# Two halves of a linear layer, walked together instead of one after the other

## The chip, the cores and the metric

The kernel runs on one core of one Trainium2 chip. The metric is device time in microseconds of one execution. A profiled execution of the same program gives the trace from which the rows below are read.

## The reference, cut to what matters

For each of 64 batch entries a 64 x 64 matrix W is picked out of 16 by an index, and mixes the 64 channels of x (1024 long). The result y goes through a linear layer with a weight that is stored as 6-bit numbers, four of them in three words, and x is added at the end:

```python
W = weights[condition]                                # 64 of 16 matrices, 64 x 64
y = jnp.einsum('bct,bcd->bdt', x, W)                  # x: 64 x 64 x 1024
w = (unpacked.astype(jnp.float32) - zero_point) * scale   # 1024 x 1024, a scale and zero point per row
out = x + jnp.einsum('bsk,nk->bsn', y, w) + bias
```

## The kernel before

Two batch entries make a tile of 128 rows, so there are 32 tiles, numbered t = i * 4 + j in loops of RING = 4. For each tile the engines do the following.

- SyncE (SP) loads x and, by the two indices, the mixing matrices (`reload`, seven tiles ahead in the steady part), and stores the two halves of the outputs (`store`), which wait for `o_ready[h]`.
- TensorE runs the mix (`mix`, L249): eight chunks of x as stationary operand against a block-diagonal matrix, into y_ps. It appears as 16 matmuls in the trace. A small sum follows (`sum_y`, L262, two short matmuls). Then comes the linear layer.
- ScalarE copies y_ps to y_hi, rounded (L355), and VectorE subtracts to get the rest, y_lo (L434). Both halves of the number are multiplied with the weight, so that little precision is lost. ScalarE also sums x (L346); POOL adds the bias to x (L540); VectorE adds the zero point's share (`residual`, L443).
- VectorE finishes a half of the outputs with two instructions: it scales o_ps into o_sb (`scale_out`, L454), which sets the semaphore `scaled[h]`, and adds the residual (`add_residual`, L462), which sets `o_ready[h]`. In each tile it does half 0 first, then half 1.

The linear layer (`linear` and `products`, L274 to L288) multiplies the eight chunks of y with qT, 1024 wide, in two halves of 512 outputs (H = 2), each of which fills one bank of o_ps. A half walks all eight chunks, each with y_hi and y_lo: 16 matmuls, with the piece of y as stationary operand and 512 columns of qT moving. Half 0 waits for the tile's y_lo and for `scaled[0]` of the tile before, half 1 for `scaled[1]` of the tile before. A matmul's data type is fp32r; each `nc.tensor.matmul` asks for a load of its stationary operand and a matmul.

The order on TensorE is written out by hand. A warm-up of 20 matmuls (L300) is followed by a prologue in which mixes, transposes of the weight (L270) and the first linears alternate. In the steady part, `step` (L290) does the mix and the sum of the tile three ahead and then the linear of tile j, both halves. The last steps (L330) have no mix left from tile 29 on; tile 31 does half 0 and then two quarter-wide pieces (`last_pieces`, L334). y_ps has two buffers, o_ps has one per half, o_sb has two, and x, y_hi, y_lo and resid have four.

Of the kernel before, what the change touches and what calls it, by code (L numbers as in the profile page):

```python
# [31 lines left out]
def adaln_ffn(nc: bass.Bass, x, cond, weights, qweight, scale, zero, bias, out):  # L32
    B, C, K = x.shape
    NCOND, _, S = weights.shape
    N, KP = qweight.shape
    assert C == S == P // 2 and N == K
    G = KP // 3
    KT = K // P
    NT = N // P
    H = 2  # L40
    NH = N // H
    TILES = B // 2
    RING = 4
# [8 lines left out]
    with ExitStack() as ctx:  # L52
        def sb(name, shape, dt):
            return ctx.enter_context(nc.sbuf_tensor(name, shape, dt))

        def psum(name, shape, dt):
            return ctx.enter_context(nc.psum_tensor(name, shape, dt))

        def sem(name):
            return ctx.enter_context(nc.semaphore(name))  # L60
# [5 lines left out]
        y_hi = sb("y_hi", [P, RING, KT, P], F32R)  # L66
        y_lo = sb("y_lo", [P, RING, KT, P], F32R)
        qT = sb("qT", [P, KT, N], F32R)
# [16 lines left out]
        o_ps = psum("o_ps", [P, H, NH], F32)  # L85
# [31 lines left out]
        y_lo_ready = sem("y_lo_ready")  # L117
# [5 lines left out]
        o_ps_ready = [sem(f"o_ps_ready{h}") for h in range(H)]  # L123
        scaled = [sem(f"scaled{h}") for h in range(H)]
# [5 lines left out]
        def x_arrived(eng, j, i):  # L130

            eng.wait_ge(x_loaded[j % RING], (i + j // RING + 1) * 16)
# [3 lines left out]
        def _(sp):  # L136
# [36 lines left out]
            def store_last():  # L173
                t = TILES - 1
                store(t % RING, t // RING, 0)
                for n, (_, col, width) in enumerate(last_pieces):
                    sp.wait_ge(o_ready[1], t + 1 + n)
                    sp.dma_start(out_rows[t * P:(t + 1) * P, col:col + width],
                                 o_sb[:, t % 2, col:col + width]).then_inc(o_stored[1][t % 2], 16)
# [58 lines left out]
        @block.tensor  # L238
        def _(pe):
            def mix(j, i):  # L240

                t = i * RING + j
                slot = j % RING
                x_arrived(pe, j, i)
                pe.wait_ge(w_loaded[slot], (i + j // RING + 1) * 32)
                if not isinstance(t, int) or t >= 2:
                    pe.wait_ge(y_lo_ready, (t - 1) * 2)
                for kt in range(KT):
                    last = nc.tensor.matmul(y_ps[:, j % 2, kt, :], x_sb[:, slot, kt * P:(kt + 1) * P],  # L249
                                            w_sb[:, slot, :], start=True, stop=True)  # L250
                    if kt % (KT // 2) == KT // 2 - 1:
                        last.then_inc(y_ps_ready, 1)

            def sum_y(j, i):

                t = i * RING + j
                slot = j % RING
                pe.wait_ge(w_stacked[slot], (i + j // RING + 1) * 32)
                pe.wait_ge(xsum_ready, t * 2 + 2)
                if not isinstance(t, int) or t >= 1:  # L260
                    pe.wait_ge(ysum_ready, t * 2)
                nc.tensor.matmul(ysum_ps[0:S, 2 * slot:2 * slot + 2], w_stack[:, slot, :], xsum[:, slot, :],  # L262
                                 start=True, stop=True).then_inc(ysum_ps_ready, 1)

            def transpose_q(n):
                pe.wait_ge(q_cast, n + 1)
                if n >= 2:
                    pe.wait_ge(qt_ready, n - 1)
                for kt in range(KT):
                    last = nc.tensor.transpose(qt_banks[n % 2][:, kt, :], q_bf[:, n % 4, kt * P:(kt + 1) * P],  # L270
                                               ident[:])
                last.then_inc(qt_ps_ready, 1)

            def linear(j, i, h):  # L274
                t = i * RING + j
                if h == 0:
                    pe.wait_ge(y_lo_ready, t * 2 + 2)
                if not isinstance(t, int) or t >= 1:
                    pe.wait_ge(scaled[h], t)
                products(o_ps[:, h, :], h * NH, NH, j % RING).then_inc(o_ps_ready[h], 1)  # L280

            def products(bank, col, width, slot):
                for kt in range(KT):
                    for part in (y_hi, y_lo):
                        last = nc.tensor.matmul(bank, part[:, slot, kt, :], qT[:, kt, col:col + width],  # L285
                                                start=(kt == 0 and part is y_hi),
                                                stop=(kt == KT - 1 and part is y_lo))
                return last  # L288

            def step(j, i, mixes=True):  # L290
                if mixes:
                    mix(j + LEAD, i)
                    sum_y(j + LEAD, i)
                for h in range(H):
                    linear(j, i, h)


            pe.wait_ge(warm_ready, 1)
            for _ in range(WARMUP):
                nc.tensor.matmul(ysum_ps[:], warm[:, 0:P], warm[:], start=True, stop=True)  # L300
            mix(0, 0)
            sum_y(0, 0)
            pe.wait_ge(ident_ready, 1)
            for n in range(NT // 2):
                transpose_q(n)
            mix(1, 0)
            pe.wait_ge(qt_ready, NT // 2)
            linear(0, 0, 0)
            sum_y(1, 0)
            mix(2, 0)  # L310
            sum_y(2, 0)
            transpose_q(4)
            transpose_q(5)
            linear(1, 0, 0)
            transpose_q(6)
            transpose_q(7)
            linear(2, 0, 0)
            mix(3, 0)
            sum_y(3, 0)
            pe.wait_ge(qt_ready, NT)  # L320
            for j in range(3):
                linear(j, 0, 1)
                mix(j + RING, 0)
                sum_y(j + RING, 0)
            for h in range(H):
                linear(3, 0, h)
            with pe.Fori(1, TRIPS - 1) as i:
                for j in range(RING):
                    step(j, i)
            for j in range(RING - 1):  # L330
                step(j, TRIPS - 1, mixes=j + LEAD < RING)
            linear(RING - 1, TRIPS - 1, 0)
            pe.wait_ge(scaled[1], TILES - 1)
            for bank, col, width in last_pieces:  # L334
                products(bank, col, width, RING - 1).then_inc(o_ps_ready[1], 1)
# [235 lines left out]
```

## Time and profile before

| | us |
|---|---|
| median of 3 runs | 331.95 |
| lowest, highest | 331.39, 332.85 |
| span of the profiled execution (first to last instruction) | 331.5 |
| TensorE matmuls busy | 319.6 |
| TensorE loads busy | 268.9 |
| VectorE busy | 211.4 |
| ScalarE busy | 127.8 |
| POOL busy | 78.3 |

The profiled execution's own time is not listed beside its span. Engine names in the rows: PE is TensorE's matmuls and PEld its loads of stationary operands, which overlap; DVE is VectorE, ACT is ScalarE, POOL is GpSimd, SP is SyncE. The start of a matmul is recorded and its end is modelled, so the distance of two starts says more than a length. L285 is the linear's matmul, L249 that of the mix. PEclk is the granted TensorE clock as a share of 2.4 GHz.

### The profile page before, as it was taken

How to read it: one execution, taken by the hardware profiler on the slowest of the kernel's cores; microseconds unless marked ns; L12 is line 12 of the kernel's file. 1: busy time of each engine (PE TensorE's matmuls, PEld its weight loads, DVE VectorE, ACT ScalarE, POOL GpSimd, SP SyncE). 2: the span in 40 equal slices, each digit the busy share in tenths (PEclk: the TensorE clock that was granted, in tenths of full speed). 3: DMA queues.
4: the chain of work that ended last, by engine and by line, in shares of the span. 5: the costliest groups of instructions: out<-in, count | busy, mean ns of one | idle time of the engine just before them, and what ended most of it. 6: DMA issues, size and time to landing. Idle time of an engine off the chain costs nothing.

```text
span 331.5 us, 5520 instructions
## 1 busy us (share of the span) xinstructions
PE 319.6 (96%) x1700; PEld 268.9 (81%) x1700; DVE 211.4 (64%) x262; ACT 127.8 (39%) x265; POOL 78.3 (24%) x39
## 2 busy tenths in 40 slices
PE   8797699999999999999999999999999999999995
PEld 3685588888888888888888888888888888888885
DVE  3459984666566676665666766656667666566563
ACT  4659157543333444433334444333344443330000
POOL 1006505222112222221122222211222222112000
PEclk9779599999999999999999999999999999999999
DMA  5895055625333333233333332433333321111112
GB/s 174 237 317 190 10 176 166 199 83 198 125 114 104 131 132 104 100 134 122 115 116 117 132 111 94 135 121 116 115 119 130 109 96 63 55 40 65 63 73 86
DMA packets 25805, 40.52 MB, mean 122 GB/s; under 512 B 11970, under 2 KB 12226, under 8 KB 25794
## 3 DMA queue, kind: packets, MB, share of 16 engines
q1 hardware_dynamic: 25794, 40.39, 36.5%
q8 instruction: 5, 0.08, 0.1%
q14 instruction: 6, 0.05, 0.0%
HBM read 23.59 MB, written 16.78 MB: 122 GB/s over the span
## 4 chain that ended last, share of the span: by engine, by line
PE 91%; DVE 3%; SPq 2%; DMA 1%; ACT 1%; issue 1%
PE o_ps L285 71%; PE y_ps L249 17%; PE ysum_ps L262 2%; DMA q_raw<-in_L_ffn_qweight_dram 1%; DVE q_bf L426 1%; DVE q_int L419 1%; DVE q_int L421 1%; ACT junk L346 1%; PE o_ps L270 1%; PE y_ps L285 1%; SPq L182 0%; SPq L148 0%; SPq L153 0%; SPq L144 0%; SPq L139 0%
## 5 line engine op out<-in xcount | busy, mean ns | idle before, releaser
L285 PE MATMUL o_ps<-qT,y_hi 128*128 128x512 f32 (+1 forms) x512 | 203.7, 399 | 0.0
L285 PE MATMUL o_ps<-qT,y_lo 128*128 128x512 f32 (+1 forms) x512 | 199.5, 390 | 0.0
L540 POOL TENSOR_TENSOR resid<-x_sb,bias_bc 128x1024 f32<-128x1024 f32 x32 | 77.1, 2414 | 221.6 <-DVE o_sb L462 195.7
L285 PEld LDWEIGHTS o_ps<-qT,y_hi 128*128 128x128 f32 x512 | 97.1, 190 | 20.0
L285 PEld LDWEIGHTS o_ps<-qT,y_lo 128*128 128x128 f32 x512 | 97.2, 190 | 19.1
L454 DVE TENSOR_TENSOR o_sb<-o_ps,scale_bc 128x512 f32<-128x512 f32 x63 | 43.6, 691 | 92.8 <-PE o_ps L285 92.8
L355 ACT ACTIVATE y_hi<-y_ps 128x512 fp32r<-128x512 f32 x64 | 38.2, 599 | 157.6 <-PE y_ps L249 157.6
L346 ACT ACTIVATE junk<-x_sb 64x1024 bf16<-64x1024 f32 x64 | 67.6, 1057 | 1.6
L249 PEld LDWEIGHTS y_ps<-w_sb,x_sb 128*128 128x128 f32 x512 | 63.6, 196 | 2.4
L249 PE MATMUL y_ps<-w_sb,x_sb 128*128 128x128 f32 x512 | 64.1, 280 | 0.0
L443 DVE SCALAR_TENSOR_TENSOR resid<-zs_bc,ysum,resid 128x1024 f32<-128x1024 f32 x32 | 60.4, 1886 | 0.0
L434 DVE TENSOR_TENSOR y_lo<-y_ps,y_hi 128x512 fp32r<-128x512 f32 x64 | 44.0, 691 | 12.0 <-ACT y_hi L355 9.1
L462 DVE TENSOR_TENSOR o_sb<-o_sb,resid 128x512 f32<-128x512 f32 x63 | 43.6, 692 | 2.3
L346 ACT ACTIVATION_READ_ACCUMULATOR junk<-x_sb 64x1 f32 x64 | 11.8, 185 | 0.0
L365 ACT ACTIVATE ysum<-ysum_ps 64x1 f32<-64x1 f32 x64 | 10.1, 158 | 2.3 <-PE ysum_ps L262 1.5
L262 PEld LDWEIGHTS ysum_ps<-xsum,w_stack 128*64 128x64 f32 x64 | 6.1, 134 | 5.0 <-issue 1.4
L262 PE MATMUL ysum_ps<-xsum,w_stack 128*64 128x2 f32 x64 | 8.8, 207 | 0.8 <-issue 0.8
L417 DVE TENSOR_SCALAR q_int<-q_raw 128x256 int16<-128x256 int16 x8 | 3.7, 459 | 7.8 <-DMA q_raw<-in_L_ffn_qweight_dram 7.8
L300 PE MATMUL ysum_ps<-warm 128*128 128x512 bf16 x20 | 7.0, 530 | 1.2 <-DVE warm L470 1.2
L270 PE MATMUL o_ps<-ident,q_bf 128*128 128x128 bf16 x32 | 3.3, 265 | 4.9 <-DVE q_bf L426 4.9
L270 PEld LDWEIGHTS o_ps<-ident,q_bf 128*128 128x128 bf16 x32 | 2.5, 119 | 5.3 <-DVE q_bf L426 5.3
L300 PEld LDWEIGHTS ysum_ps<-warm 128*128 128x128 bf16 x20 | 2.5, 129 | 5.2 <-issue 3.3
(26 smaller groups left out, 45.3 us busy)
## 6 DMA issues: line engine op xcount, KB each, us to landing
x_sb<-in_x_dram SPq DMA_DIRECT2D x32, 512.0 KB, 3.3
out_dram<-o_sb SPq DMA_DIRECT2D x63, 256.0 KB, 2.0
q_raw<-in_L_ffn_qweight_dram SPq DMA_DIRECT2D x8, 384.0 KB, 5.4
w_sb<-in_L_cond_weights_dram SPq DMA_DIRECT2D x64, 16.0 KB, 2.0
w_stack<-in_L_cond_weights_dram SPq DMA_DIRECT2D x64, 16.0 KB, 2.1
scale_bc<-_L_ffn_weight_scale_dram SPq DMA_DIRECT2D x1, 512.0 KB, 6.1
zs_bc<-n_weight_zero_point_dram SPq DMA_DIRECT2D x1, 512.0 KB, 7.5
bias_bc<-in_L_ffn_bias_dram SPq DMA_DIRECT2D x1, 512.0 KB, 8.4
```

The source lines that it names most:

```text
L249: last = nc.tensor.matmul(y_ps[:, j % 2, kt, :], x_sb[:, slot, kt * P:(kt + 1) * P], w_sb[:, slot, :], start=True, stop=True)
L262: nc.tensor.matmul(ysum_ps[0:S, 2 * slot:2 * slot + 2], w_stack[:, slot, :], xsum[:, slot, :], start=True, stop=True).then_inc(ysum_ps_rea ...
L285: last = nc.tensor.matmul(bank, part[:, slot, kt, :], qT[:, kt, col:col + width], start=(kt == 0 and part is y_hi), stop=(kt == KT - 1 and ...
L300: nc.tensor.matmul(ysum_ps[:], warm[:, 0:P], warm[:], start=True, stop=True)
L346: nc.scalar.activation(junk[rows, :], x_sb[rows, j % RING, :], ACT.Copy, accum_out=xsum[rows, j % RING, half:half + 1]).then_inc(xsum_read ...
L355: nc.scalar.activation(y_hi[:, j % RING, chunks, :], y_ps[:, j % 2, chunks, :], ACT.Copy).then_inc(y_hi_ready, 1)
L365: nc.scalar.activation(ysum[half * S:(half + 1) * S, j % RING:j % RING + 1], ysum_ps[0:S, col:col + 1], ACT.Copy).then_inc(ysum_ready, 1)
L434: nc.vector.tensor_tensor(y_lo[:, j % RING, chunks, :], y_ps[:, j % 2, chunks, :], y_hi[:, j % RING, chunks, :].bitcast(F32), ALU.subtract ...
L443: nc.vector.scalar_tensor_tensor(resid[:, j % RING, :], zs_bc[:], ysum[:, j % RING:j % RING + 1], resid[:, j % RING, :], ALU.mult, ALU.add ...
L454: nc.vector.tensor_tensor(o_sb[:, j % 2, cols], o_ps[:, h, :], scale_bc[:, cols], ALU.mult).then_inc(scaled[h], 1)
L462: nc.vector.tensor_tensor(o_sb[:, j % 2, cols], o_sb[:, j % 2, cols], resid[:, j % RING, cols], ALU.add).then_inc(o_ready[h], 1)
L540: nc.gpsimd.tensor_tensor(resid[:, j % RING, :], x_sb[:, j % RING, :], bias_bc[:], ALU.add).then_inc(xbias_ready, 1)
```

## The change

A new function, `linear_both`, takes the place of two calls of `linear` in the steady steps and for tile 3. It waits for y_lo and for both `scaled` semaphores first, then walks the chunks once: at each chunk and for each of y_hi and y_lo it issues the matmul of half 0 and then that of half 1, with the same stationary operand. The last matmul of each half sets that half's `o_ps_ready`. Tiles 3 to 30 go through it; tiles 0 to 2 and tile 31 keep `linear` and `products`.

```diff
--- before.py
+++ after.py
@@ -271,6 +271,21 @@
                                                ident[:])
                 last.then_inc(qt_ps_ready, 1)
 
+            def linear_both(j, i):
+                t = i * RING + j
+                pe.wait_ge(y_lo_ready, t * 2 + 2)
+                for h in range(H):
+                    pe.wait_ge(scaled[h], t)
+                for kt in range(KT):
+                    for part in (y_hi, y_lo):
+                        for h in range(H):
+                            last = nc.tensor.matmul(o_ps[:, h, :], part[:, j % RING, kt, :],
+                                                    qT[:, kt, h * NH:(h + 1) * NH],
+                                                    start=(kt == 0 and part is y_hi),
+                                                    stop=(kt == KT - 1 and part is y_lo))
+                            if kt == KT - 1 and part is y_lo:
+                                last.then_inc(o_ps_ready[h], 1)
+
             def linear(j, i, h):
                 t = i * RING + j
                 if h == 0:
@@ -291,8 +306,7 @@
                 if mixes:
                     mix(j + LEAD, i)
                     sum_y(j + LEAD, i)
-                for h in range(H):
-                    linear(j, i, h)
+                linear_both(j, i)
 
 
             pe.wait_ge(warm_ready, 1)
@@ -322,8 +336,7 @@
                 linear(j, 0, 1)
                 mix(j + RING, 0)
                 sum_y(j + RING, 0)
-            for h in range(H):
-                linear(3, 0, h)
+            linear_both(3, 0)
             with pe.Fori(1, TRIPS - 1) as i:
                 for j in range(RING):
                     step(j, i)
```

## Rows read from the trace of the kernel before

**Rows 1.** Page, table of engines: busy us, share of the span, instructions.
```profile
PE 319.6 (96%) x1700; PEld 268.9 (81%) x1700; DVE 211.4 (64%) x262; ACT 127.8 (39%) x265; POOL 78.3 (24%) x39
```

**Rows 2.** Chain of waits, steady part: start us, length us, what, how many instructions.
```profile
201.93 1.78 PE y_ps L249 x16
...
203.93 7.48 PE o_ps L285 x32
211.41 1.78 PE y_ps L249 x16
```

**Rows 3.** Timeline of TensorE, one tile: start us, length us, engine, line, operation.
```profile
196.33 0.39 PE L285 MATMUL o_ps<-qT,y_hi 128*128 128x512 f32 x1
...
197.92 0.39 PE L285 MATMUL o_ps<-qT,y_lo 128*128 128x512 f32 x1
198.15 0.39 PE L285 MATMUL o_ps<-qT,y_hi 128*128 128x512 f32 x1
...
201.54 0.39 PE L285 MATMUL o_ps<-qT,y_lo 128*128 128x512 f32 x1
```

**Rows 4.** Timeline of all engines at that tile's end; in brackets idle time and releaser.
```profile
201.97 0.69 DVE L454 TENSOR_TENSOR o_sb<-o_ps,scale_bc 128x512 f32<-128x512 f32 x1 [2.21 <-PE o_ps L285]
202.70 0.69 DVE L462 TENSOR_TENSOR o_sb<-o_sb,resid 128x512 f32<-128x512 f32 x1
...
203.49 0.69 DVE L434 TENSOR_TENSOR y_lo<-y_ps,y_hi 128x512 fp32r<-128x512 f32 x1
203.53 2.40 POOL L540 TENSOR_TENSOR resid<-x_sb,bias_bc 128x1024 f32<-128x1024 f32 x1 [7.07 <-DVE o_sb L462]
...
203.85 0.50 PE L285 MATMUL o_ps<-qT,y_hi 128*128 128x512 f32 x1
...
204.19 0.39 PE L285 MATMUL o_ps<-qT,y_lo 128*128 128x512 f32 x1
```

**Rows 5.** Timeline of VectorE, same tile and the next.
```profile
198.35 0.69 DVE L454 TENSOR_TENSOR o_sb<-o_ps,scale_bc 128x512 f32<-128x512 f32 x1 [0.81 <-PE o_ps L285]
...
205.00 2.02 DVE L443 SCALAR_TENSOR_TENSOR resid<-zs_bc,ysum,resid 128x1024 f32<-128x1024 f32 x1
```

**Rows 6.** Groups by line and form: count, busy us, mean ns, idle before.
```profile
L285 PEld LDWEIGHTS o_ps<-qT,y_lo 128*128 128x128 f32 x512 | 97.2, 190 | 19.1
...
L300 PE MATMUL ysum_ps<-warm 128*128 128x512 bf16 x20 | 7.0, 530 | 1.2 <-DVE warm L470 1.2
...
L300 PEld LDWEIGHTS ysum_ps<-warm 128*128 128x128 bf16 x20 | 2.5, 129 | 5.2 <-issue 3.3 <-DVE warm L470 1.2
...
L270 PEld LDWEIGHTS qt_ps<-ident,q_bf 128*128 128x128 bf16 x32 | 1.8, 99 | 2.1 <-DVE q_bf L426 1.8 <-issue 0.3
```

**Rows 7.** Timeline of VectorE early on, independent instructions in a row.
```profile
41.11 0.69 DVE L462 TENSOR_TENSOR o_sb<-o_sb,resid 128x512 f32<-128x512 f32 x1
41.72 1.28 DVE L443 SCALAR_TENSOR_TENSOR resid<-zs_bc,ysum,resid 128x1024 f32<-128x1024 f32 x1
```

**Rows 8.** Timeline of all engines, TensorE waiting for VectorE's cast.
```profile
13.75 0.43 DVE L426 TENSOR_SCALAR q_bf<-q_int 128x1024 bf16<-128x1024 int16 x1
...
14.23 0.13 PEld L270 LDWEIGHTS o_ps<-ident,q_bf 128*128 128x128 bf16 x2 [0.94 <-DVE q_bf L426]
```

**Rows 9.** Chain of waits, last four tiles.
```profile
298.66 27.53 PE o_ps L285 x128
```

**Rows 10.** Timeline of TensorE's loads, end of the warm-up.
```profile
6.30 1.40 PEld L300 LDWEIGHTS ysum_ps<-warm 128*128 128x128 bf16 x7 [0.28 <-issue]
```

**Rows 11.** Timeline of TensorE, a long idle stretch in the prologue.
```profile
35.70 0.61 PE L270 MATMUL o_ps<-ident,q_bf 128*128 128x128 bf16 x4 [4.18 <-DVE q_bf L426]
```

**Rows 12.** Windows of 1 us: length, busy of each engine, PEclk, DMA share, GB/s.
```profile
33.00:34.00 1.00, 0.00 (x0) 0.00 (x0) 0.96 (x2) 0.00 (x0) 1.00 (x1) 0.81 0.26 86
...
35.00:36.00 1.00, 0.30 (x4) 0.30 (x4) 1.00 (x2) 0.00 (x0) 1.00 (x2) 0.50 0.10 20
...
40.00:41.00 1.00, 1.00 (x5) 0.76 (x4) 1.00 (x1) 0.00 (x0) 0.00 (x0) 0.78 0.00 0
```

## The prediction

> **What bounds the kernel now.** I began with the page's table of engines: TensorE's matmuls are busy 96% of the span and its loads 81% [rows 1]. Ends of matmuls are modelled, so the share alone does not say that TensorE is the bound. The chain of waits does: in the steady part it holds nothing but TensorE, 7.48 us of linear (32 matmuls), then the mix and its small sum, then the next linear [rows 2]; one tile takes 9.48 us (211.41 against 201.93). Next I read the timeline of one tile for two things: how far apart matmuls start, and when VectorE empties the two banks of o_ps.
>
> Spacing: from 196.33 to 201.54 lie 23 steps, 0.2265 us each [rows 3]. The step from the first half's last matmul (197.92, bank 0, first columns of qT) to the second half's first (198.15, bank 1, other columns) is 0.23, like its neighbours.
>
> Emptying: call the start of a tile's last linear matmul S, here 201.54. VectorE's scaling of the second half starts at 201.97, S + 0.43, and its addition 0.73 later [rows 4]. The first half's last matmul starts at 197.92, and its scaling starts at 198.35, again 0.43 later [rows 5]. So today bank 0 is emptied beside 16 matmuls on bank 1, and bank 1 beside the mix; the next linear starts at 203.85, S + 2.31 [rows 4], and waits for neither.
>
> **The change, part by part.**
>
> Work of TensorE. Matmuls, columns and requested loads stay the same in number; only their order changes. In 28 tiles (3 to 30) each piece of y is now used by two matmuls in a row, 28 x 16 = 448 pairs. The price of a matmul whose stationary operand is already in the array is not in the trace for this data type. Bounds: 512 columns at the full 2.4 GHz last 0.2133 us, so at most 0.0132 us could go from each of 896 matmuls, 11.8 us. At the other end nothing goes, and no reason lets the shared load cost more; switching bank and columns costs nothing by the step at 198.15, though at every step rather than once a tile. I take zero. The nearest row is the warm-up: 20 matmuls with one stationary operand, and the profile lists 20 loads [rows 6], so a repeated operand was loaded again each time; and in the linear a load of 0.19 us runs beside the matmul before it already [rows 6].
>
> The Trainium skill, "TensorE: Matmul & The Clock Gate", section "Back-to-back issue gap", gives 518 cycles at 2.4 GHz, 216 ns, for 512 columns of an isolated matmul. The warm-up agrees; the linear is some 10 ns above it. Were that the gap of every shared matmul, the sum would fall by the amount in the first rival.
>
> Waits. Until now the first half waited for bank 0, the second for bank 1. Now the first matmul of a tile waits for both, and both banks finish together: bank 0 at S - 0.23, bank 1 at S. Behind the wait stands all of TensorE's linear, and behind that everything. VectorE's chain, on the same tile: scaling of half 0 at 201.54 - 0.23 + 0.43 = 201.74; its addition 0.73 later, 202.47; scaling of half 1 0.61 after that, the distance of an addition to an instruction that waits for nothing [rows 7], 203.08; its end 0.69 later, 203.77. From VectorE's end to TensorE's load there are 0.05 us (13.75 + 0.43 = 14.18, load at 14.23) [rows 8]: 203.82. Today's linear starts at 203.85. So where a mix lies between two linears, the chain is hidden by 0.03 us, a near tie: cost 0 for the 25 such transitions (into tiles 4 to 28). The price cannot be below 0, since TensorE waits for nothing there now. Above: if the second scaling came 0.73 after the addition as a dependent instruction does, each transition would cost 0.09, 25 x 0.09 = 2.3 us. If it came after 0.79, as today's y_lo piece at 203.49 does, which waited for ScalarE [rows 4], 0.15, 25 x 0.15 = 3.8 us. I keep 0 to 3.8 and take 0: that scaling depends on nothing unfinished, so the row of the unhindered step is the nearest.
>
> The tail. Tiles 29 to 31 have no mix in front; the chain shows tiles 28 to 31 as one block of 128 linear matmuls [rows 9]. Nothing covers the chain there. Into tiles 29 and 30 the first matmul starts at S + 2.28 instead of S + 0.23: 2.05 lost. Its second matmul follows after 0.34 (203.85 to 204.19) instead of 0.23, since its load has no matmul to hide beside [rows 4]: 0.11 more. 2 x 2.16 = 4.3 us. Tile 31 keeps the old order and waits only for bank 0 of tile 30: 201.74 + 0.69 + 0.05 = 202.48, S + 0.94 against S + 0.23, 0.71 plus 0.11 = 0.8 us. Bank 1 is free 3 us before its turn. Tail: 5.1 us.
>
> What moves on other engines. VectorE's second addition ends some 1.1 us later (chain 203.08 + 0.61 + 0.69 = 204.4, today 202.70 + 0.69 = 203.39), so y_lo, the residual and POOL's bias addition (released at 203.53 today) start about 1.1 us later, and SP's next reload, which waits for POOL, with them. Each is needed one tile or more later: the residual, 205.00 to 207.02 today [rows 5], would end near 208.1, and its next reader is the chain at 211.2. The y_lo pieces are read two mixes on. First-half stores go out 3.4 us later in SP's queue, beside their twins; o_sb is reused two tiles (19 us) later. All at 0; if this cover were gone, the mix or linear behind would wait that 1.1 us per tile, but the slacks are 3 us and more.
>
> Sum: 0 + 0 + 5.1. The profiled span of 331.5 would be 336.6. What lay around it in that execution is not listed; the median of the three timed runs, 331.95, is 0.5 above the span, and 331.95 + 5.1 = 337.1 us.
>
> **The rivals.**
>
> 1. The sharing pays (not slower). If a repeated load is dropped, or costs the array nothing, the second matmul of a pair may start after the warm-up's spacing. There the last seven loads take 1.40 us; less the last one's 0.10 (the mean of such a load in the transposes) six steps remain, 0.217 each [rows 6, 10]. 0.2265 - 0.217 = 0.0095, x 448 = 4.3 us: 337.1 - 4.3 = 332.8, no change. If both of a pair gain, 8.5 us: 328.6, faster. For it: the linear's step is longer than 512 columns need. Against: the warm-up repeats its loads and still has the short step, so data type may be what differs. Decides from 0.0077 us per pair, where the result comes within 0.5%.
>
> 2. The near tie is lost in every tile. For it: 0.03 us is within what I added up from two-decimal rows. Against: each link is a row. Price 2.3 to 3.8 us: 339.4 to 340.9. The Trainium skill, "Perfetto Trace Analysis", section "Optimizing Tensor Performance", wants independent groups rotated through banks so that emptying one overlaps the next group. No row here shows it failing yet; the change gives that overlap up in every tile, which is where this rival would begin.
>
> 3. TensorE's clock falls in the tail. For it: after 31.52, when TensorE went idle for 4.18 us [rows 11], the granted clock reached 0.81 in 33 to 34, so it fell to its lower level at 33.6, 2.1 us into the idle time; 35.70 to 40.4 then ran at 1.2 GHz [rows 12]. The tail's two idle stretches are 1.9 us (S + 0.39 to S + 2.28). Against: they are shorter and lie between linears of over 7 us without a hole. One fall costs half of 4.7 us, 2.4: 339.5; two, 341.9.
>
> **How the numbers follow.** Forecast 0.55 (336.3 to 338.0 by itself: the tail with or without small errors of 0.8 us). Sharing pays 0.20, of which 0.06 end faster and 0.14 within 0.5% (1.7 us, about what a measurement here can tell from no change). Near tie lost 0.13. Clock 0.12. So faster 0.06, same 0.14, slower 0.80. The range reaches down to the first rival's 332.8 less 0.3 and up to 341.0, which leaves out two clock falls and a gain by both of a pair.
>
> **What would show it.** Right: still 1700 loads, linear steps of 0.2265, the first linear matmul at S + 2.31 in the steady part, and a new row in the list of waits, TensorE for L454 on VectorE, three times, some 4.5 us in all, the longest about 1.9. Wrong: fewer loads or two alternating spacings (rival 1); 25 or more short waits on L454 and tiles longer than 9.47 (rival 2); a clock below 1.00 after 300 us (rival 3). If the tail shows no waits I have misread the order.

## The result, and the profile after

The change makes the kernel slower: 341.34 us (339.63 to 342.31, 4 runs) against 332.4 (331.39 to 332.93, 4 runs), a ratio of 1.027 [1.0225, 1.0311]. Forecast were 337.1, at most 341.0. The side was right, the size was not: 8.9 us instead of 5.1. In every run here the time lies 1.8 us above the span, so the execution whose trace stood ahead of the prediction (span 331.5) will have taken some 333.3 and was one of the longer ones; I had set its span beside the median.

The page's first section, of the changed kernel:

```profile
PE 320.1 (95%) x1700; PEld 267.6 (79%) x1700; DVE 215.0 (64%) x262; ACT 127.7 (38%) x265; POOL 79.5 (24%) x39
```

There are still 1700 loads for 1700 matmuls [rows 1]. The groups by line and form (count, busy us, mean ns, idle before) show that each matmul of a pair loads its own copy:

```profile
L282 PE MATMUL o_ps<-qT,y_lo 128*128 128x512 f32 x448 | 138.3, 390 | 0.0
L282 PEld LDWEIGHTS o_ps<-qT,y_lo 128*128 128x128 f32 x448 | 84.1, 188 | 17.9
```

448 matmuls on y_lo, 448 loads of it: two per piece, 188 ns each (190 before [rows 6]). Nothing was shared but the address.

The end of a steady tile, timeline of all engines; the last linear matmul starts at S = 201.72:

```profile
201.72 0.39 PE L282 MATMUL o_ps<-qT,y_lo 128*128 128x512 f32 x1
...
201.92 0.69 DVE L467 TENSOR_TENSOR o_sb<-o_ps,scale_bc 128x512 f32<-128x512 f32 x1 [3.09 <-PE o_ps L282]
...
202.65 0.69 DVE L475 TENSOR_TENSOR o_sb<-o_sb,resid 128x512 f32<-128x512 f32 x1
...
203.26 0.68 DVE L467 TENSOR_TENSOR o_sb<-o_ps,scale_bc 128x512 f32<-128x512 f32 x1
...
203.83 0.28 PE L262 MATMUL ysum_ps<-xsum,w_stack 128*64 128x2 f32 x2
...
204.06 0.30 PEld L282 LDWEIGHTS o_ps<-qT,y_hi 128*128 128x128 f32 x2
204.09 0.70 PE L282 MATMUL o_ps<-qT,y_hi 128*128 128x512 f32 x2
```

VectorE's chain is the one that was summed up: S + 0.20, + 0.73, + 0.61. The small sum is issued at 203.83, but the second scaling ends at 203.26 + 0.68 = 203.94, and the linear's first matmul starts only at 204.09, 0.15 after that end: S + 2.37 instead of S + 2.31 [rows 4]. The tile after it, same view:

```profile
211.24 0.39 PE L282 MATMUL o_ps<-qT,y_lo 128*128 128x512 f32 x1
...
211.53 0.69 DVE L467 TENSOR_TENSOR o_sb<-o_ps,scale_bc 128x512 f32<-128x512 f32 x1 [3.23 <-PE o_ps L282]
...
212.87 0.68 DVE L467 TENSOR_TENSOR o_sb<-o_ps,scale_bc 128x512 f32<-128x512 f32 x1
...
213.70 0.70 PE L282 MATMUL o_ps<-qT,y_hi 128*128 128x512 f32 x2
```

Here the first scaling comes 0.29 after S, not 0.20, and the linear starts at S + 2.46. The two kinds alternate through the whole steady part.

The tail, chain of waits (start us, length us, what):

```profile
299.57 7.31 PE o_ps L282 x31
306.88 0.02 issue
306.90 0.70 DVE o_sb L467
...
307.63 0.04 DVE o_sb L475
...
308.24 0.69 DVE o_sb L467
308.93 0.14 issue
309.07 7.29 PE o_ps L282 x31
...
326.61 0.14 issue
326.74 4.34 PE o_ps L300 x20
```

Where the chain held one block of 128 matmuls [rows 9], it now runs from linear to VectorE and back: scaling, the start of an addition, scaling, and 0.14 of "issue" ahead of the next linear; into tile 31 one scaling and the same 0.14. The list of waits (waiting operation, releaser: us in total, times, longest) has the new row:

```profile
PE o_ps L300 <- DVE o_sb L467: 5.4, 2, 4.8
...
PE o_ps L282 <- DVE o_sb L467: 4.0, 2, 2.0
```

4.0 us are the two holes in front of tiles 29 and 30; of the other row 0.6 is tile 31 and the rest belongs to the prologue.

Adding up this trace from the start of tile 2's last linear matmul (59.45 before, 58.61 after) to the end of the span: 272.0 before, 279.2 after. That is 7.2 us: 1.8 over the 25 steady transitions (into tiles 4 to 28) and 5.4 in the tail. The same stretch will be used below. The timings say 8.9, so 1.7 us were not in this trace.

### The profile page after: what moved, and what is told of

Read it like the earlier page. It is cut to its first block, busy times and chain, and to the rows that moved or that the text cites. A ratio compares the mean times of both kernels' runs of the same rounds, so it can differ in the third digit from the quotient of the medians.

```text
span 337.8 us, 5520 instructions
## 1 busy us (share of the span) xinstructions
PE 320.1 (95%) x1700; PEld 267.6 (79%) x1700; DVE 215.0 (64%) x262; ACT 127.7 (38%) x265; POOL 79.5 (24%) x39
## 4 chain that ended last, share of the span: by engine, by line
PE 88%; DVE 6%; issue 2%; SPq 2%; DMA 1%; DVEq 0%
PE o_ps L282 62%; PE y_ps L249 16%; PE o_ps L300 7%; PE ysum_ps L262 2%; DVE o_sb L467 2%; DVE resid L456 1%; DMA q_raw<-in_L_ffn_qweight_dram 1%; DVE zs_bc L499 1%; DVE zs_bc L497 1%; PE y_ps L300 1%; PE o_ps L270 0%; DVE y_lo L447 0%; SPq L148 0%; SPq L153 0%; SPq L144 0%
## 5 line engine op out<-in xcount | busy, mean ns | idle before, releaser
L282 PE MATMUL o_ps<-qT,y_hi 128*128 128x512 f32 x448 | 140.5, 395 | 4.9 <-DVE o_sb L467 4.0
L282 PE MATMUL o_ps<-qT,y_lo 128*128 128x512 f32 x448 | 138.3, 390 | 0.0
L553 POOL TENSOR_TENSOR resid<-x_sb,bias_bc 128x1024 f32<-128x1024 f32 x32 | 78.4, 2453 | 222.4 <-DVE o_sb L475 196.3
L282 PEld LDWEIGHTS o_ps<-qT,y_hi 128*128 128x128 f32 x448 | 81.9, 188 | 22.6 <-issue 4.7
L456 DVE SCALAR_TENSOR_TENSOR resid<-zs_bc,ysum,resid 128x1024 f32<-128x1024 f32 x32 | 75.0, 2343 | 0.0
L447 DVE TENSOR_TENSOR y_lo<-y_ps,y_hi 128x512 fp32r<-128x512 f32 x64 | 41.3, 683 | 3.5 <-ACT y_hi L368 3.3
L300 PE MATMUL o_ps<-qT,y_hi 128*128 128x512 f32 (+1 forms) x64 | 25.7, 407 | 5.4 <-DVE o_sb L467 5.4
L300 PE MATMUL o_ps<-qT,y_lo 128*128 128x512 f32 (+1 forms) x64 | 24.9, 395 | 0.0
L300 PEld LDWEIGHTS o_ps<-qT,y_hi 128*128 128x128 f32 x64 | 12.9, 201 | 8.4 <-DVE o_sb L467 4.8
```

The costliest lines, as they stand in the source:

```text
L282: last = nc.tensor.matmul(o_ps[:, h, :], part[:, j % RING, kt, :], qT[:, kt, h * NH:(h + 1) * NH], start=(kt == 0 and part is y_hi), stop= ...
L447: nc.vector.tensor_tensor(y_lo[:, j % RING, chunks, :], y_ps[:, j % 2, chunks, :], y_hi[:, j % RING, chunks, :].bitcast(F32), ALU.subtract ...
L456: nc.vector.scalar_tensor_tensor(resid[:, j % RING, :], zs_bc[:], ysum[:, j % RING:j % RING + 1], resid[:, j % RING, :], ALU.mult, ALU.add ...
L553: nc.gpsimd.tensor_tensor(resid[:, j % RING, :], x_sb[:, j % RING, :], bias_bc[:], ALU.add).then_inc(xbias_ready, 1)
```

## The experiments

The theories: A, all that is lost are the linear's waits for VectorE's scaling, in the steady part and in the tail; B, the new order costs something more wherever it runs; C, in part of the executions the clock falls in the tail; D, the remainder is chance in the kernel's start. Times are medians, each against the kernel before on the same chip.

**The changed kernel again.** No edit.

> The changed kernel once more, to size the whole effect. Theory A: all that is lost are waits of the linear's first matmul for VectorE's scaling, 1.8 us over the 24 steady transitions and 5.4 us in the three last ones, so the true difference is about 7.1 us and the 8.9 us of the first timing holds 1.8 us of chance from the start of the kernel, which varies from run to run. Rival B: the new order costs a further 1.8 us at a place that the span does not show, in every run: 8.9 us again.

340.71 against 331.84, ratio 1.026 [1.0231, 1.0293]: 8.9 us again, with an interval of 7.7 to 9.7, so the remainder is no accident of one timing. The trace gave 279.2 for the stretch, as the first one. A alone, 7.1, lies outside the interval. (The steady transitions are 25, not 24: into tiles 4 to 28.)

**The old order in tiles 29 and 30 only.**

```diff
...
-                linear_both(j, i)
+                if both:
+                    linear_both(j, i)
+                else:
+                    for h in range(H):
+                        linear(j, i, h)
...
+                step(j, TRIPS - 1, mixes=j + LEAD < RING, both=j == 0)
```

> The new order in tiles 3 to 28, the old one in tiles 29 and 30. Theory A: the steady transitions still lose 1.8 us; into tile 29 the first half waits for the first scaling of tile 28 alone, 0.9 us; the rest of the tail loses nothing: 2.7 us over the kernel before. Rival B (a cost of the order itself, wherever it runs): 1.8 us more, 4.5 us. Had the tail nothing to do with it, it would be as slow as the changed kernel, 7 to 9 us over.

335.23, ratio 1.0087 [1.0062, 1.0113]: +3.4. In the trace the stretch took 274.7, +2.7, as A has it to a tenth. B as put here is out: 26 tiles in the new order and no 1.8 us on top in the trace, and its 4.5 lies outside the interval of the timings (2.1 to 3.8).

**The new order in tiles 29 and 30 only** (`both=j > 0` in the last steps, the old calls everywhere else).

> The old order in tiles 3 to 28, the new one in tiles 29 and 30 only. Theory A: into tile 29 the linear waits for one scaling (second half of tile 28), about 1.1 us, into tile 30 for the whole chain, 2.2 us, into tile 31 for one scaling, 0.9 us: 4.2 us over the kernel before, the steady part unchanged at 9.47 us a tile. Rival B: no more than that either, since only two tiles have the new order; so with the run before it B would leave a remainder that A does not.

337.26, ratio 1.0148 [1.0124, 1.0172]: +5.4; the trace's stretch 276.3, +4.3 against the 4.2 expected, and steady tiles of 9.47. Again the trace agrees with A and the timing lies 1.1 higher; its interval, 4.1 to 5.7, just takes in A.

**Waiting for bank 1 one matmul later.**

```diff
-                for h in range(H):
-                    pe.wait_ge(scaled[h], t)
+                pe.wait_ge(scaled[0], t)
...
+                            if h == 1 and kt == 0 and part is y_hi:
+                                pe.wait_ge(scaled[1], t)
```

> The new order everywhere, but the first matmul of a tile waits for bank 0 only, and the wait for bank 1 stands before the second matmul. Theory A: in the steady part bank 0 is free at S + 1.0, bank 1 at S + 2.4 to 2.5, the second matmul was due at S + 2.65: no wait is left, 9.47 us a tile. In the tail the first matmul starts at S + 1.0 and the second at S + 2.4: 2.0 us in each of two transitions and 0.9 us in the last, 4.9 us over the kernel before. Rival B: 1.8 us more than that, 6.7 us.

337.42, ratio 1.0172 [1.0144, 1.0199]: +5.6. In the trace the steady tile is back at 9.47 with the first matmul at S + 2.31, and the stretch takes 276.9, +4.9, as A has it. By the trace the interleaved order by itself is free; the wait in front of it is what costs. Of the timings' interval, 4.8 to 6.6, A's 4.9 is inside and B's 6.7 just outside. The chain of waits in front of tile 29's second matmul also shows what a wait at the head of the linear adds:

```profile
306.24 0.70 DVE o_sb L468
306.94 0.04 issue
306.98 7.12 PE o_ps L283 x30
```

From VectorE's end to TensorE 0.04, near the 0.05 of [rows 8]. At the head of a linear in the tail the same view shows 0.14, whether one scaling is awaited or two. Being at the head is not the difference: in the changed kernel's prologue the first matmul of tile 1's second half starts at 47.18, 0.06 after VectorE's end. What differs in the traces is where the wait stands. In the short cases the load itself waits for VectorE's semaphore. At the 0.14 heads the load waits for y_lo, and the scalings are awaited by an instruction of their own ahead of it (EVENT_SEMAPHORE, line 278 of the changed kernel, or 294 where one scaling is awaited; 51 ns each): in front of tile 29 VectorE ends at 308.92, that instruction runs from 308.96 to 309.01, the load starts at 309.04 and the matmul at 309.07.

**Nine matmuls to fill the tail's holes.**

```diff
+            def fill(count):
+                for _ in range(count):
+                    nc.tensor.matmul(qt_ps[:, :, :].rearrange("p t n -> p (t n)").bitcast(F32), warm[:, 0:P], warm[:],
+                                     start=True, stop=True)
...
+                else:
+                    fill(9)
```

The `else` belongs to `if mixes` in `step`, so the fillers stand where there is no mix.

> The changed kernel, with nine further matmuls of 512 columns on the warm-up's tile in front of the linears of tiles 29 and 30, into a bank that nothing else uses by then. Nine take 1.9 us, which fits into the wait of 2.1 us, so that the linear starts when it did, but TensorE is not idle before it. The traces so far show a difference of 7.2 us between the end of tile 2 and the end of the kernel, the timings 8.9. Theory C: in the executions without a trace the clock often fell in one of the idle stretches of the tail; then filling them brings the median to about 339.0, 7.2 over the kernel before, and narrows its spread. Theory D: the 1.7 us come from the start of the kernel; then the median stays at 340.7.

339.43 (339.15 to 340.1), ratio 1.0221 [1.0192, 1.025]: +7.4 (interval 6.4 to 8.3), where the changed kernel had 8.9 (7.7 to 9.7, on another chip), and a spread of 1.0 us where it had 2.9. That is what C expects; under D alone the median would have stayed. The spread is the weaker sign: the kernel before, which has no hole in its tail, spreads by 2.9 us on this chip. Chain of waits and windows of 2 us (length, busy of each engine, PEclk, DMA share, GB/s):

```profile
307.39 1.96 PE qt_ps L307 x9
309.35 0.02 issue
309.37 7.54 PE o_ps L282 x32
```

```profile
308.00:310.00 2.00, 1.98 (x10) 0.97 (x8) 1.97 (x4) 0.00 (x0) 0.00 (x0) 1.00 0.26 99
310.00:312.00 2.00, 2.00 (x11) 1.61 (x10) 1.14 (x1) 0.00 (x0) 0.00 (x0) 1.00 0.44 163
```

The fillers end at 309.35 and the linear starts at 309.37, 2.37 after S as without them; the wait is still there, TensorE just does not stand idle in it. The stretch takes 279.3 and the clock stays at 1.00.

**Three single executions of the changed kernel.** No edit.

> The changed kernel once more, for the trace of an execution. Theory C, where this execution takes over 340.3: the granted clock falls to 0.5 after one of the idle stretches of the tail (305 to 330 us), linear steps there are 0.427 us for some microseconds, and from the end of tile 2 to the end it takes more than 279.2. Where it takes less: 279.2 and a clock of 1.00 throughout the tail. Against it: a slow execution with a clock of 1.00 in the tail.

> As the run before it, another execution: over 340.3 with a clock that falls in the tail, or below with one that does not.

> As the two runs before it, another execution: over 340.3 with a clock that falls in the tail, or below with one that does not.

341.68, 341.74 and 340.89. The first two show it. Windows of the first, tail:

```profile
306.00:308.00 2.00, 0.05 (x1) 0.08 (x1) 1.93 (x4) 0.00 (x0) 0.00 (x0) 1.00 0.00 0
308.00:310.00 2.00, 2.00 (x7) 1.63 (x8) 1.73 (x2) 0.00 (x0) 0.00 (x0) 0.77 0.66 247
310.00:312.00 2.00, 2.00 (x6) 1.51 (x6) 0.00 (x0) 0.00 (x0) 0.00 (x0) 0.50 0.04 15
312.00:314.00 2.00, 2.00 (x10) 1.63 (x9) 0.00 (x0) 0.00 (x0) 0.00 (x0) 0.88 0.00 0
...
318.00:320.00 2.00, 0.96 (x3) 0.84 (x4) 1.97 (x4) 0.00 (x0) 0.00 (x0) 0.83 0.35 131
```

and its timeline of TensorE (pairs with one operand are grouped):

```profile
308.49 0.63 PE L282 MATMUL o_ps<-qT,y_lo 128*128 128x512 f32 x2
308.96 0.93 PE L282 MATMUL o_ps<-qT,y_hi 128*128 128x512 f32 x2
309.69 1.05 PE L282 MATMUL o_ps<-qT,y_lo 128*128 128x512 f32 x2
310.54 1.05 PE L282 MATMUL o_ps<-qT,y_hi 128*128 128x512 f32 x2
```

TensorE idles from 305.97 to 307.95, the linear starts, and by the share of 0.77 the clock falls at 309.1, to 1.2 GHz; pairs then take 0.85 us (309.69 to 310.54) instead of 0.45. It is back at about 312.5. The same follows the second hole (0.83 in 318 to 320). Tiles 29 and 30 end 11.09 us apart instead of 9.5: 1.6 us each, 3.2 together, and the stretch takes 282.3 (282.5 in the second execution). The third missed its expectation: over 340.3, yet the stretch is 279.2 and the clock 1.00 in the tail, which is D's case; its start was late (tile 2's last matmul at 59.8, against 57.5 and 57.4), with the clock low from about 13 to 19 and 47 to 53. So in the traces the fall came in 2 of 5 executions, in both holes or in none, and the start of the kernel varies besides, by over 2 us. The two that fell are the two with the shortest start (the others: 58.6 to 59.8); whether that is chance, five executions do not say. Of the filled kernel's six timings none has room for both falls: 340.1 less 1.8 less 282.5 would leave 55.8 for the start.

**VectorE scales both halves before it adds.**

```diff
+            def finish_both(j, i):
+                for h in range(H):
+                    scale_out(j, i, h)
+                for h in range(H):
+                    add_residual(j, i, h)
```

> The changed kernel, with VectorE scaling both halves of a tile before it adds the residual to either. Theory A: both banks are free at S + 1.6 to 1.8 instead of S + 2.4 to 2.5. In the steady part the linear starts at S + 2.31 as before the change: 9.47 us a tile, nothing lost. In the tail 1.5 us are lost into each of tiles 29 and 30 and 0.9 into tile 31: 3.9 us over the kernel before, 335.7. Theory C: idle stretches of 1.3 us are too short for the clock to fall, so nothing on top. Theory D: up to 1.7 us on top, 337.4.

336.6, ratio 1.0124 [1.0092, 1.0155]: +4.5. The chain of waits into tile 29:

```profile
305.39 0.03 DVE o_sb L467
...
306.00 0.69 DVE o_sb L467
306.69 0.14 issue
306.83 7.32 PE o_ps L282 x31
```

The linear starts at S + 1.64 (S = 305.19); in the steady part every tile is at S + 2.31, 9.47 us. The stretch: 276.0, +3.9, as A has it. Of the timings' interval, 3.1 to 5.1, the 3.9 of C is inside and the full 5.6 of D outside; a part of it is not excluded.

**The old order in bf16.**

```diff
-        y_hi = sb("y_hi", [P, RING, KT, P], F32R)
-        y_lo = sb("y_lo", [P, RING, KT, P], F32R)
-        qT = sb("qT", [P, KT, N], F32R)
+        y_hi = sb("y_hi", [P, RING, KT, P], BF16)
+        y_lo = sb("y_lo", [P, RING, KT, P], BF16)
+        qT = sb("qT", [P, KT, N], BF16)
...
-                                            y_hi[:, j % RING, chunks, :].bitcast(F32),
+                                            y_hi[:, j % RING, chunks, :],
```

> The kernel before, in its old order, with y_hi, y_lo and the weight qT held in bf16 instead of fp32r; y is so rounded to two bf16 parts. Two readings of the linear's step of 0.2265 us, which is 0.010 us longer than the warm-up's. If the data type makes it longer: steps of 0.216 us although every matmul has another stationary operand, 0.34 us less a tile, and 10 to 11 us less in all, 321. If changing the stationary operand makes it longer: steps stay at 0.2265 us and the time at 332; then sharing could have paid if the repeated load were dropped.

317.86, ratio 0.957 [0.9539, 0.9595]: 14.2 us faster. Timeline of TensorE, and the loads by form:

```profile
222.56 0.39 PE L285 MATMUL o_ps<-qT,y_hi 128*128 128x512 bf16 x1
222.78 0.38 PE L285 MATMUL o_ps<-qT,y_lo 128*128 128x512 bf16 x1
223.00 0.38 PE L285 MATMUL o_ps<-qT,y_hi 128*128 128x512 bf16 x1
...
225.16 0.38 PE L285 MATMUL o_ps<-qT,y_hi 128*128 128x512 bf16 x1
```

```profile
L285 PEld LDWEIGHTS o_ps<-qT,y_lo 128*128 128x128 bf16 x512 | 50.4, 98 | 56.9 <-issue 1.7
```

Ten steps from 223.00 to 225.16, 0.216 each, with another stationary operand at every one: the 0.010 us went with the data type, and in bf16 a new operand at every matmul does not lengthen the step. The type changed the load too, 98 ns instead of 190 [rows 6], so whether in fp32r a load that is really dropped would shorten the step is not shown: none was dropped. The second matmul of a tile now follows the first by 0.22 instead of 0.34 [rows 4], 0.11 more per tile, which the expectation had left out.

**Twenty matmuls in the prologue of the kernel before** (the `fill` above, after the mix of tile 4).

> The kernel before, with 20 further matmuls on the warm-up's tile in the prologue, after the mix of tile 4, where the traces show TensorE idle for some 6 us (40.9 to 47.0) and its clock at 1.2 GHz until about 51. If the idle time makes the clock fall: the linear after it runs in 3.6 us instead of 5.3, and the kernel takes 1.7 us less than before, 330.1. If the clock falls for another reason, nothing changes: 331.8.

330.09, ratio 0.9937 [0.9912, 0.9962]: 2.0 us faster (seven of eight timings from 329.32 to 330.41, one of 338.6, which the ratio leaves out). Windows between 44 and 50, of the changed kernel's second trace (same prologue, unfilled) and of this one:

```profile
44.00:46.00 2.00, 0.00 (x0) 0.00 (x0) 1.97 (x4) 1.08 (x2) 0.00 (x0) 0.75 0.23 74
46.00:48.00 2.00, 0.86 (x2) 0.77 (x3) 1.97 (x4) 1.22 (x3) 0.05 (x1) 0.50 0.59 174
48.00:50.00 2.00, 2.00 (x6) 1.52 (x6) 1.00 (x2) 0.00 (x0) 2.00 (x1) 0.50 0.67 241
```

```profile
46.00:48.00 2.00, 1.89 (x8) 1.59 (x9) 1.95 (x4) 0.17 (x2) 1.07 (x1) 1.00 0.92 317
48.00:50.00 2.00, 2.00 (x11) 1.65 (x11) 0.00 (x0) 0.00 (x0) 1.33 (x1) 1.00 0.18 56
```

Idle for 4.1 us (42.99 to 47.13), the clock falls to half; filled, it stays at 1.00. In the one trace of the kernel before, the long hole lay earlier, at 31.5 to 35.7 [rows 11], and the clock was low there instead.

**Both gains together.** The last two edits.

> The two edits that gained, together, in the old order of the linear: y and qT in bf16, and 20 further matmuls in the prologue's idle stretch. If the gains add (14.2 and 2.0 us): 315.9. If the prologue's gain shrinks because its linears are already shorter in bf16: 316 to 317.5.

316.04, ratio 0.9514 [0.9483, 0.9545]. That is 16.9 us by the medians, 15.1 to 17.2 by the interval. The sum of the gains, 16.2, lies in it and so does most of the other reading (14.6 to 16.1), so the run does not tell them apart. It is the fastest version here, in the old order, and not the same arithmetic: y is kept in two bf16 parts.

## Why the prediction was right and wrong

*Right.* Slower, and by the mechanism named: no load was saved (1700), linear steps stayed at 226 to 227 ns, and VectorE's chain came out into the open where no mix covers it. The tail was forecast at 5.1 and measured 5.4 us at full clock; the difference is 0.1 at each of three heads, the link that is wrong below. The moved work on VectorE, POOL and SP cost nothing: with the wait split, tiles are back at 9.47. One price was overlooked there: VectorE's `residual`, 2.02 us before, with 0.94 of it beside POOL's bias addition, now takes 2.52, with 1.44 beside it (1.28 where POOL is idle). The tiles of 9.47 have it too, so it cost nothing.

*Wrong, first: the near tie was taken at 0.* It was mis-sized on both links. I took 0.05 us from VectorE's end to TensorE from a transpose [rows 8]; at the head of these linears, with the separate wait in front, it is 0.15. And I read one tile's scalings, 0.43 after their matmuls [rows 4, 5], for all: in the kernel before, every second tile has its first-half scaling 0.53 after its matmul, as the next tile shows:

```profile
207.39 0.39 PE L285 MATMUL o_ps<-qT,y_lo 128*128 128x512 f32 x1
...
207.92 0.69 DVE L454 TENSOR_TENSOR o_sb<-o_ps,scale_bc 128x512 f32<-128x512 f32 x1 [0.90 <-PE o_ps L285]
```

So the linear starts 0.06 and 0.15 late by turns; its second matmul follows 0.03 sooner, and 25 transitions cost 1.8 us. The second rival, whose sign (tiles longer than 9.47) is there, gave 2.3 to 3.8 for it.

*Wrong, second: the clock in the tail was taken at 0.* The third rival had the place right, but was given 0.12, because the holes (1.9 us) were shorter than the idle time after which the clock had fallen in the prologue (2.1 us). That one value was no limit: the same trace has a fall at 13.1, to 0.50 until 20.0, where no idle stretch before it was over 1.6 us,

```profile
12.79 0.76 PE L270 MATMUL qt_ps<-ident,q_bf 128*128 128x128 bf16 x8 [1.60 <-DVE q_bf L426]
```

```profile
13.00:14.00 1.00, 0.55 (x8) 0.29 (x5) 0.97 (x4) 0.41 (x1) 0.00 (x0) 0.57 0.63 166
```

and in the changed kernel's five traces the long hole of the prologue had lasted 1.8 to 4.9 us when the clock fell. In the tail, in two of five traces it fell at both holes, 1.1 and 0.3 us after the linear had restarted. Its price was 1.6 us a fall, not 2.4. The filled tail puts what the clock takes from the median at 1.5 us (8.9 less 7.4, each known to about 1 us); by the traces it is 3.2 in two executions of five, 1.3 on average.

Sum as measured: 1.8 + 5.4 + about 1.5 = 8.7, of 8.9 us, where the last term is itself a difference of timings and so no check of its own. Forecast: 0 + 5.1 + 0. The second timing's median, 340.71, would have lain just below the upper end, 341.0, and the first, 341.34, just above; either way the sum was short by 3.6 us and more. Each missing term had been priced as a rival by itself; their sum, 5.1 + 2.3 + 4.8 by my own prices, would have reached past the upper end of the range, which I had built from one rival at a time.

*The first rival* (sharing pays) is out: no load was dropped and the step stayed. The bf16 run shows the short step without sharing.

*Left open.* Whether the 0.09 of the separate wait would go if the load itself waited for the scaling was not tried. The medians of four variants lie 0.6 to 1.1 above what their traces add up to, all within their intervals; the start varies by more than that. The clock may have fallen in some of their executions, which no trace of theirs shows, and two of them (old order in 29 and 30; wait split) have no hole over 0.8 us in the tail. A further cost of the new order of under 1 us is not excluded there; the filled kernel, 7.4 by the timings and 7.3 by its trace, shows none.

## What to carry to other kernels

Two matmuls in a row on one stationary operand saved nothing here, where the profile lists a load for each and the load already runs beside a matmul; look at the count of loads first. An order that closes two banks together also opens them together: sum up the evacuation of both against the work that lies between, at the place with the least of it, which here was the tail without mixes. One idle stretch after which the clock fell is not the shortest after which it falls: look for others in the same trace. When several rivals with one sign can hold at once, the end of the range is their sum.

## What the runs showed of the hardware

- Holes of 2.0 us in front of a tile, between dense linears of 7.3 us, let the clock fall to 1.2 GHz in two traced executions of the same program and not in three others; with nine matmuls into an unused bank before each linear it stayed at 1.00 in the one trace, and none of six timings has room for two falls.
- A matmul of 512 columns starts every 226.5 ns in fp32r and every 216 ns in bf16, each with its own load of 188 to 190 and 98 ns.
- The Trainium skill, "TensorE: Matmul & The Clock Gate", section "Back-to-back issue gap", gives 518 cycles at 2.4 GHz, 216 ns, for 512 columns of an isolated matmul, and less, some 131 ns, for a stream of loads and matmuls. The bf16 rows are such a stream and take the 216 ns; no row here shows the lower figure. The fp32r rows are some 10 ns longer still. The measurement decides.
- Behind VectorE's end, a matmul whose load waits for it starts after 0.04 to 0.06 us; with a separate wait instruction of 51 ns in front of the load, after 0.14 to 0.15.
- VectorE's `residual` over 128 x 1024 takes 1.28 us with POOL idle, 2.02 with 0.94 us beside POOL's bias addition and 2.52 with 1.44 beside it.
